# Linear attention on one core: states kept in tiles of four heads, one batch per turn of the loops, one buffer for q features and values

## What is computed

```python
qkv = x @ W_qkv + b_qkv
q = elu(q * E ** -0.5) + 1.0001        # E = 8, per head
k = elu(k) + 1.0001
for t in range(L):                     # a scan over the 512 tokens
    kv_s = kv_s + outer(k_t, v_t)      # 8 x 8 per head
    k_s = k_s + k_t
    out_t = (q_t @ kv_s) / (q_t . k_s + 1e-6)
out = out @ W_out + b_out
```

## Time and profile before

| | us |
|---|---|
| median of 3 runs | 605.54 (605.45 to 606.7) |
| the profiled execution | 610.65 |
| its span, first to last instruction | 608.9 |
| busy in it: PE, PEld | 444.8, 297.6 |
| busy: DVE, ACT, POOL | 345.6, 237.6, 331.3 |

### The profile page before, as it was taken

The page is one execution under the profiler, slowest core; times in us unless marked ns, Lnnn a source line. Parts: engine busy times, 40 slices in busy tenths (PEclk is TensorE's granted clock), DMA queues, the critical chain, the costliest instruction groups (busy, mean ns, idle before and its releaser), DMA issues.

```text
span 608.9 us, 12872 instructions
## 1 busy us (share of the span) xinstructions
PE 444.8 (73%) x4788; PEld 297.6 (49%) x4788; DVE 345.6 (57%) x984; ACT 237.6 (39%) x629; POOL 331.3 (54%) x259
## 2 busy tenths in 40 slices
PE   1884966997699325899999979149867599857970
PEld 1742543553345213677777768148335355433440
DVE  6396971221115992687777865485999222212097
ACT  4971212332224277555555530187611133322420
POOL 6184776888786601222222220004987788887691
PEclk9987875555569657799999986656978555555995
DMA  8998600101009980001111110541000000100592
GB/s 267 375 250 323 232 9 9 9 5 10 7 5 377 408 317 0 2 3 39 36 34 35 34 36 10 156 177 57 2 0 9 8 8 6 10 6 6 174 409 107
DMA packets 34389, 60.40 MB, mean 99 GB/s; under 512 B 12611, under 2 KB 18846, under 8 KB 33870
## 3 DMA queue, kind: packets, MB, share of 16 engines
q1 hardware_dynamic: 23078, 58.41, 26.8%
q0 software_dynamic: 11264, 1.38, 2.6%
HBM read 37.43 MB, written 29.36 MB: 110 GB/s over the span
## 4 chain that ended last, share of the span: by engine, by line
DVE 29%; PE 29%; issue 15%; DMA 13%; ACT 7%; POOL 5%; SPq 1%; POOLq 0%; DVEq 0%; another core or an unknown queue 0%; ACTq 0%
DVE X L973 9%; DMA rows_d<-A 5%; PE bank L897 5%; PE bank L778 4%; PE bank L878 4%; PE bank L795 3%; POOL planes_d L438 3%; DVE Cb L1075 3%; ACT A L508 3%; DMA planes_d<-Bb,put_i 2%; POOL A L452 2%; DVE bn L978 2%; DMA Bb<-planes_d 2%; PE bank L768 2%; PE bank L788 2%
## 5 line engine op out<-in xcount | busy, mean ns | idle before, releaser
L438 POOL DMA_INDIRECT planes_d<-Bb,put_i x64 | 100.4, 1569 | 24.6 <-issue 18.4
L452 POOL DMA_INDIRECT A<-rows_d,tok_i x64 | 71.9, 1124 | 20.6 <-issue 16.6
L1105 DVE TENSOR_TENSOR ring<-ring,bank 128x88 f32<-128x88 f32 x64 | 15.7, 246 | 103.7 <-ACT ring L576 72.0
L675 PE MATMUL bank<-ident,A 128*128 128x128 f32 x96 | 22.5, 412 | 55.1 <-ACT A L508 40.9
L479 POOL TENSOR_TENSOR Bb<-Cb,chm 128x576 f32<-128x576 f32 x16 | 19.0, 1220 | 66.8 <-DVE Cb L1139 33.4
L768 PE MATMUL bank<-ident,A 128*128 128x128 f32 x64 | 30.0, 469 | 29.3 <-DMA A<-rows_d,tok_i 23.2
L396 POOL TENSOR_TENSOR Bb<-Eb,st 128x512 f32<-128x512 f32 x8 | 8.9, 1112 | 74.7 <-DVE st L1023 74.7
L570 ACT ACTIVATE ring<-bank 128x128 f32<-128x128 f32 x64 | 17.7, 277 | 81.4 <-PE bank L768 70.7
L675 PEld LDWEIGHTS bank<-ident,A 128*128 128x128 f32 x96 | 18.2, 220 | 58.1 <-issue 29.9
L479 POOL TENSOR_TENSOR Bb<-w3s,chm 128x576 f32<-128x576 f32 x16 | 17.8, 1147 | 49.8 <-PE bank L920 49.8
L795 PE MATMUL bank<-w2s,ring 88*64 88x128 f32 x256 | 43.9, 446 | 0.0
(11 more groups left out here) (155 smaller groups left out, 1121.6 us busy)
## 6 DMA issues: line engine op xcount, KB each, us to landing
planes_d<-zeros SPq DMA_DIRECT2D x8, 2048.0 KB, 20.6
w3s<-in_w3T SPq DMA_DIRECT2D x2, 2816.0 KB
rows_d<-A SPq DMA_DIRECT2D x8, 512.0 KB, 11.5
A<-planes_d SPq DMA_DIRECT2D x8, 512.0 KB, 9.2
PL<-planes_d SPq DMA_DIRECT2D x8, 512.0 KB, 10.1
Cb<-planes_d SPq DMA_DIRECT2D x8, 512.0 KB, 10.8
Bb<-planes_d SPq DMA_DIRECT2D x8, 512.0 KB, 12.0
w1s<-in_w1T SPq DMA_DIRECT2D x1, 2816.0 KB
```

The source lines that it names most:

```text
L438: pool.indirect_dma_start(out=planes_d[f], in_=Y[:, s, :], in_offset=None, out_offset=bass.IndirectOffsetOnAxis(ap=put_i[:, s:s + 1], axis=0),
L452: pool.indirect_dma_start(out=A[:, t, :], out_offset=None, in_=rows_d, in_offset=bass.IndirectOffsetOnAxis(ap=tok_i[:, t:t + 1], axis=0), ...
L675: ins = pe.transpose(bank[g % 2][:, (i % 4) * P:(i % 4 + 1) * P], A[:, i, :], ident[:, :])
```

## The change

It does five things, all in the attention stage.

1. States are computed in tiles of four heads. For each q and c there are four matmuls, j = 0 to 3, of 32 k features (heads 4j to 4j + 3) against the GW = 36 v columns of the same four heads. Tile j lands on partitions 32j to 32j + 31. SW has 36 columns instead of 144 for each q and c. The state of a whole quarter fits in one bank; two banks are used, 0 and 1, and bank 2 no longer.
2. The products with earlier states are four times 15 matmuls with 32 rows of q features and 36 columns, in place of two times 15 with 128 rows and 72 columns. They read their own copy of the q features, QI, which ScalarE makes (a new instruction, after the four of `split_q`).
3. The outputs lie in banks 4 to 7, four heads in each, and each group of four heads waits for its own masked scores. The four banks are one PSUM tensor `upper`, and VectorE normalises all of it in three instructions in place of six.
4. There is one buffer for q features and one for values. `value(b + 1)` stands at the end of VectorE's step, before the wait for the outputs, and waits for GpSimd's products and the state products of batch b.
5. The loops have one batch in their body.

```diff
-    NH = 2 * NQ
-    STATES = (0, 2, 1)
-    AFTER = ((), (0, 1, 2), (3, 4), (5, 6, 7))
+    GW = 4 * (E + 1)
+    STATES = (0, 1)
+    AFTER = ((), (0, 1), (2,), (3,))
...
+        SW = Cb[:, 0:NQ * NC * GW].rearrange("p (q c v) -> p q c v", q=NQ, c=NC)
+        VN = Cb[:, o:o + NQ * VW].rearrange("p (q h f) -> p q h f", q=NQ, h=HEADS)
...
+        bank = [ctx.enter_context(nc.psum_tensor(f"bank{k}", [P, 512], F32)) for k in range(4)]
+        upper = ctx.enter_context(nc.psum_tensor("upper", [P, 4, 512], F32))
+        bank += [upper[:, k, :] for k in range(4)]
...
# ScalarE, split_q
                 for j in range(4):
-                    act.activation(Q4[:, j, :], QT[par], ACT.Copy, scale=hm[:, j:j + 1]).then_inc(q4_ready, 1)
+                    act.activation(Q4[:, j, :], QT, ACT.Copy, scale=hm[:, j:j + 1]).then_inc(q4_ready, 1)
+                act.wait_ge(o_ps, PRIMED + b)
+                act.activation(QI, QT, ACT.Copy).then_inc(qi_ready, 1)
...
# TensorE, step
-                        if last:
-                            pe.wait_ge(v_ready, b + 1)
-                        else:
-                            pe.wait_ge(v_ready, b + 2)
+                        pe.wait_ge(v_ready, b + 1)
+                        if not last:
                             pe.wait_ge(q_read, 2 * (b + 2))
                             pe.wait_ge(k_read, 2 * (b + 2))
-                    for m in AFTER[g]:
-                        q = m // 2
-                        if m >= len(STATES):
-                            pe.wait_ge(kv_sb, PRIMED + NH * b + m + 1 - len(STATES))
-                        for k in range(1 if m == NH - 1 else 2):
-                            ins = pe.matmul(bank[STATES[m % len(STATES)]][:, k * VW:(k + 1) * VW], KN[:, 2 * (m % 2) + k, q, :],
-                                            VN[par][:, q, :, :].rearrange("p h f -> p (h f)"), start=True, stop=True)
+                    for q in AFTER[g]:
+                        if q >= len(STATES):
+                            pe.wait_ge(kv_sb, PRIMED + NQ * b + q + 1 - len(STATES))
+                        for c in range(NC if q < NQ - 1 else NC - 1):
+                            for j in range(4):
+                                ins = pe.matmul(bank[STATES[q % len(STATES)]][32 * j:32 * j + 32, c * GW:(c + 1) * GW],
+                                                KN[:, c, q, 32 * j:32 * j + 32],
+                                                VN[:, q, 4 * j:4 * j + 4, :].rearrange("p h f -> p (h f)"),
+                                                start=True, stop=True)
...
-                pe.wait_ge(sc_sb, 4 * b + 4)
                 for h in range(HEADS):
+                    if h % 4 == 0:
+                        pe.wait_ge(sc_sb, 4 * b + h // 4 + 1)
+                    if h == HEADS - 1:
+                        pe.wait_ge(kv_sb, PRIMED + NQ * (b + 1))
+                        pe.wait_ge(sb_ready, (NQ - 1) * (b + 1))
+                        pe.wait_ge(qi_ready, b + 1)
...
-                for half in range(2):
+                for g in range(4):
+                    rows = slice(32 * g, 32 * g + 32)
...
+                            before_c = SW[rows, q, c - 1, :] if c else SW[rows, q - 1, NC - 1, :]
+                            o = c * GW
+                            ins = pe.matmul(bank[4 + g][32 * q:32 * q + 32, o:o + GW], QI[rows, t0:t0 + CHUNK],
+                                            before_c, start=False, stop=True, skip_group_check=True)
...
-            with pe.Fori(0, (B - 2) // 2) as i:
-                step(2 * i + 1, 1)
-                step(2 * i + 2, 0)
+            with pe.Fori(0, B - 2) as i:
+                step(i + 1)
...
# VectorE, value, q_feature and step
-                if not (isinstance(b, int) and b < 2):
-                    dve.wait_ge(vx_ready, PRIMED + NC * (b - 1))
-                    dve.wait_ge(kv_ps, PRIMED + NH * (b - 1))
+                if not (isinstance(b, int) and b == 0):
+                    dve.wait_ge(vx_ready, PRIMED + NC * b)
+                    dve.wait_ge(kv_ps, PRIMED + NQ * b)
...
+                feature(b, 0, EQ, RQ, QT, (qi_ready, n))
...
                 if not last:
-                    value(b + 1, 1 - par)
-                    q_feature(b + 1, 1 - par)
+                    q_feature(b + 1)
...
+                        dve.tensor_tensor(SW[:, q, 0:n, :].rearrange("p c (j f) -> p c j f", j=4),
+                                          bank[STATES[q % len(STATES)]][:, 0:n * GW].rearrange("p (c j f) -> p c j f", c=n, j=4),
+                                          hm[:, :].unsqueeze(1).unsqueeze(3).broadcast_to([P, n, 4, E + 1]),
+                                          ALU.mult).then_inc(kv_sb, 1)
...
                 if not first:
                     project_bias(b - 1)
+                if not last:
+                    value(b + 1)
                 dve.wait_ge(o_ps, PRIMED + b + 1)
```

More of the change, by code:

```diff
@@ L635, in copy_anT, with step @@
                 act.activation(AT, bank[3][:, :], ACT.Copy).then_inc(anT_sb, 1)
-            def step(b, par, first=False, last=False):
+            def step(b, first=False, last=False):
                 if not last:
@@ L650, in _ @@
             slice_h(1)
-            split_q(0, 0)
+            split_q(0)
             copy_kn(0)
-            step(0, 0, first=True)
-            with act.Fori(0, (B - 2) // 2 - 1) as i:
-                step(2 * i + 1, 1)
-                step(2 * i + 2, 0)
-            step(B - 3, 1)
-            step(B - 2, 0)
-            step(B - 1, 1, last=True)
+            step(0, first=True)
+            with act.Fori(0, B - 3) as i:
+                step(i + 1)
+            step(B - 2)
+            step(B - 1, last=True)
             copy_anT(B - 1)
@@ L1120, in _ @@
             norm(1)
-            for v in VN:
-                then(dve.memset(v, 1.0))
+            then(dve.memset(VN, 1.0))
             for s in (q_ready, k_ready, kv_sb, oo_ready):
@@ L1206, in _ @@
-            value(0, 0)
-            q_feature(0, 0)
-            k_feature(0)
-            step(0, 0, first=True)
-            with dve.Fori(0, (B - 2) // 2) as i:
-                step(2 * i + 1, 1)
-                step(2 * i + 2, 0)
-            step(B - 1, 1, last=True)
+                ob = upper[:, :, 0:NC * GW].rearrange("p g (n f) -> p g n f", f=E + 1)
+                den = top8[:, 0:8, :].rearrange("p a b -> p (a b)")
+                rec = top8[:, 8:16, :].rearrange("p a b -> p (a b)")
@@ L1214, in _ @@
+            value(0)
+            q_feature(0)
+            k_feature(0)
+            step(0, first=True)
+            with dve.Fori(0, B - 2) as i:
+                step(i + 1)
+            step(B - 1, last=True)
             project_bias(B - 1)
```

96 lines of the change are left out of this document (36 added, 60 removed).

## The result

The changed kernel takes **598.8 us** (median of 4 runs, 597.73 to 600.45) against 605.6 before: 0.9886 of it, interval 0.9857 to 0.9915. That is 6.8 us gained; 23.5 were forecast. The time lies inside the range of 576 to 601, but near its end. The profiled execution took 599.64 us, 0.8 above its median, where that of before was 5.1 above. So the two profiles differ by 11.2 us of span. Where before's profiled execution lost its 5.1 us is not known, and I compare stretches inside the attention stage, not whole times.

The account below looks back on a forecast made before the run. TensorE bounds the attention stage, with ScalarE's and VectorE's chains just behind. Savings of 19.3, 3.3 and 5.5 make 28.1 us, less 4.4 for one clock fall 23.7, giving 582 us; range 576 to 601 (0.8 in all).

Parts of the forecast that it names:

- minus 2.64 per batch: State products (L897) on TensorE: 120 narrow rows take 1.5 us per batch instead of 4.14.
- The products with earlier states: 0: L920 on TensorE: 60 narrower matmuls take 1.2 us as today, no difference; upper end plus 2.6 per batch.
- minus 0.59: Before the transposition of K: TensorE's 0.59 us wait for VectorE's output bias vanishes in each batch.
- without that cover 0.5 per batch: ScalarE's added copy of q (QI) hides behind the transposition of K; uncovered it costs 0.5 us per batch.
- A batch is 12.61 us: Attention stage: a batch falls from 15.82 to 12.61 us, 3.21 less.
- Six batches save 19.3. The first batch saves 3.3.: Attention stage: six batches save 19.3 us; the first saves 2.64 and its 0.68 wait for state sums, 3.3.
- 5.5: Last batch, at half clock: 2.64 become 4.9 us saved, with the 0.59 wait 5.5.
- I allow for one such fall: One added clock fall in a stretch of scores and states (5.1 us), costing 4.4 us: gain 28.1 becomes 23.7.
- Both stretches were busy with matmuls on part of the array: Claim about half-clock stretches in the last attention batch and expert stage, used to expect that narrow work lowers the clock.
- the clock falls in many batches: Rival, attention batches: three further clock falls cost 13 us (595), five cost 22 (604); chance 0.27, from 588 to 604.
- the 32 by 32 form: Rival, products with earlier states: the form costs what the scores do, 21 us more, 603; half of that 592; chance 0.08.
- issue binds: Rival, states and state products: 25 ns per narrow row instead of 9.8, a batch 15.9 us, total 610; chance 0.03.

Follow-up runs that it names:

- split scores: Kernel before, each score matmul of 128 columns written as four of 32 (192 matmuls more a batch): 692.24 us, ratio 1.1304.
- halved products: Changed kernel with 30 products with earlier states a batch instead of 60, each twice as wide, results partly wrong: 587.83 us, ratio 0.9708.
- loop of seven or eight turns: Changed kernel with batch 0 moved into TensorE's loop (seven turns): 592.19 us, ratio 0.9794; with all eight batches in it: 590.55 us, ratio 0.9665.
- before with the filled wait: Kernel before with three unused projections on TensorE in its wait at the head of the last batch: 599.61 us, ratio 0.989.
- loop of eight: Changed kernel with all eight batches in TensorE's loop, no batch's code ahead of or behind it: 590.55 us, ratio 0.9665.

## Why the prediction was right about a batch and wrong about the sum

- *The state products, "minus 2.64 per batch".* Right: 1.42 us where 1.5 was taken, so 2.72. The group L909's 9.8 ns a row was the right one to go by.
- *"The products with earlier states: 0".* Right: 1.16 against 1.20. 120 rows of 36 columns took what 60 of 72 had taken; here I was right to go by L909 and not by the scores.
- *VectorE, "minus 0.59".* Right: L845 has no wait in any settled batch.
- *ScalarE, the hidden copy, "without that cover 0.5 per batch".* Right on both counts, 0.60 uncovered. What I didn't see is that the clock can fall behind this little wait, as in two of four batches, so the cover was worth some 2 us a batch and not 0.5.
- *"A batch is 12.61 us".* 12.64.
- *"Six batches save 19.3. The first batch saves 3.3."* **This is the step that failed.** It took the saving of a batch that has run before for all of them. Batch 0 lost 2.7 instead of saving 3.3, the first turn of the loop lost 3.3 instead of saving 3.2, and the next saved 1.4 because the half clock reached into it. That is 14.3 us missing. The sum had no term for the supply of code, and a cold pass is bound by it: 748 instructions at 256 in some 4 us are 11.7 us, under the 15.8 of a batch before, and stayed hidden there (its issue waits in the stage are 0.4 us, behind the loop's jump back); 1048 are 16.4, over 12.6. The split scores show the supply by itself, the halved products and the loop of seven or eight turns show that these batches come back when instructions are fewer or passed fewer times.
- *The last batch, "5.5".* 2.0. The state products saved 5.7 there (7.96 to 2.28 from start to start), more than the 4.9 forecast. The rest took 3.7 back: the code is cold (1.62 us of wait), and the clock stayed down from 354.2 to the end of the batch, where in the kernel before it was full again from 377.3. 3.5 us missing.
- *"I allow for one such fall", 4.4 us.* In the profile there were two in the first batches, none between 289.3 and 354.2, and that of the last batch, which lasted. They came with waits of 2.8, 2.7 and 2.7 us, and not from the narrow pieces alone: four settled batches with them ran at 1.00. The rows did not bear the reading behind it either. "Both stretches were busy with matmuls on part of the array" is wrong for the last batch, where 8.3 of the 16.3 us at half clock are L897 with 128 by 128 weights. The rival *the clock falls in many batches* was near in its time, but the narrow work was not the cause. That the time still lies in the range is luck: the range was stretched to 601 for that rival and for the 32 by 32 form, and what filled it was in neither.
- *The rival "issue binds"* was priced with a constant 25 ns a row and set aside by L909's rows, which stand in a settled turn. They could not speak for a first pass. That the kernel before has code loads in its first batches was in its DMA view, and I had not read it. From 246 to 294.1 us that view of the kernel before has

```profile
q8 instruction: 9, 0.15, 1.3%
```

  and from 294.1 to 357.4 it has none. That row would have pointed at the missing term, blocks of 16 KB in cold batches only. It would not have given the size: the kernel before never waited long for one, so the pace of some 4 us was not to be read from it.

The sum 28.1, less the 14.3 and 3.5, is 10.3, what the stage gained in the profile (10.1). The 3.3 us from there to the medians' 6.8 lie outside the stage (ahead of the first transposition of K and behind the last output projection), and their cause is open: there before's profiled execution took 470.0 us, that of before with the filled wait 464.9, and the two of the changed kernel 468.9 and 468.3. Either before's profiled execution was long there, or the changed kernel loses something there; two profiles of each can't tell. How much of a cold batch's loss is the missing code and how much the clock that falls behind the wait can't be split cleanly: in batch 0 of the first profile 5.1 of 6.6 us are waits; in the loop of eight the second batch has no wait at all and still takes 15.09, 2.4 more than a settled one, all of it clock. Why a block takes about 4 us is open, and no run has a loop's body between 1500 and 3030 instructions.

## What to carry to other kernels

Count instructions as well as columns when matmuls get narrower: code that is passed once, ahead of a loop, in its first turn or behind it, came here at about 256 instructions in 4 us, and a saving below that pace is not paid out there. Put the first and the last turn into the loop, even with some unused work, as long as the body stays loaded (1500 instructions did here, 3030 did not). And fill a wait of a few us on TensorE ahead of a busy stretch: three unused matmuls gained 1.1% in the kernel before, about as much as this change.

## What the runs showed of the hardware that was not expected

- TensorE's code comes in 16 KB loads, seven in 34.9 us and 22 in 90, one every 4.1 to 5 us; from one stop to the next stand 127 or 128 rows, once 249. The Trainium skill (Runtime: NRT & Kernel Launch, Instruction fetch mechanics) gives blocks of 16 KiB or 256 instructions and room for 2048 instructions of TensorE, and both agree with these runs: bodies of 1050 and 1500 stayed, 3030 did not. It also says that fetching is hidden because instructions are issued more slowly than they are filled. The runs do not agree: 11.3 us of issue waits in the changed kernel, 36.9 in the one with split scores.
- Idle time of 0.60 us in a narrow stretch was followed by 7 us at a clock of 0.5 in two of four batches, and the same stretch without it ran at 1.00 in all four.
- The wait of 2.71 us at the head of the last batch was followed by 16 us at 0.5 and, filled, by none: 8.1 us less in the kernel before, all clock, since the fill took as long as the wait.
